# A gated delta net whose four engines issue the same operations in another order

## The reference

```python
def step(S, inp):                       # one token, one head; S is 64 x 128
    qt, kt, vt, bt, gt = inp
    S = S * jnp.exp(gt)[..., None, None]
    kv = jnp.einsum('bhk,bhkv->bhv', kt, S)
    delta = (vt - kv) * bt[..., None]
    S = S + jnp.einsum('bhk,bhv->bhkv', kt, delta)
    ot = jnp.einsum('bhk,bhkv->bhv', qt, S)
    return (S, ot)
```

## Time and profile before

| | us |
|---|---|
| median of three runs | 5250.11 (5246.1 to 5253.67) |
| profiled execution, its own time | 5260.0 |
| its span | 5258.1 |
| PE busy in the span | 4913.4 (93%) |
| POOL, DVE, ACT busy | 3475.1, 3668.1, 3196.8 |
| mean granted TensorE clock | 0.978 of full |

### The profile page before, as it was taken

The page is one execution under the profiler, slowest core; times in us unless marked ns, Lnnn a source line. Parts: engine busy times, 40 slices in busy tenths (PEclk is TensorE's granted clock), DMA queues, the critical chain, the costliest instruction groups (busy, mean ns, idle before and its releaser), DMA issues.

```text
span 5258.1 us, 227335 instructions
## 1 busy us (share of the span) xinstructions
PE 4913.4 (93%) x99564; PEld 3489.0 (66%) x99564; DVE 3668.1 (70%) x5109; ACT 3196.8 (61%) x4833; POOL 3475.1 (66%) x3554
## 2 busy tenths in 40 slices
PE   5999999999999879999999999999999999999998
PEld 3777777777777646666666666666666666665665
DVE  3666666666666567777777777777767776777775
ACT  3666666666666546656655665666655665555554
POOL 2677667676776567666666666776666666766664
PEclk6999999999999989999999999999999999999999
DMA  1000000000000012322222223222222223222222
GB/s 47 3 3 3 8 3 3 7 3 3 3 7 3 31 48 60 81 56 61 63 78 63 65 65 85 64 60 61 59 75 56 65 64 85 64 60 65 60 66 57
DMA packets 154831, 238.86 MB, mean 45 GB/s; under 512 B 42746, under 2 KB 53368, under 8 KB 152952
## 3 DMA queue, kind: packets, MB, share of 16 engines
q1 hardware_dynamic: 153848, 224.32, 16.3%
HBM read 24.96 MB, written 4.19 MB: 6 GB/s over the span
## 4 chain that ended last, share of the span: by engine, by line
PE 77%; ACT 8%; issue 5%; DVE 4%; POOL 4%; POOLq 0%; DVEq 0%; ACTq 0%
PE banks L172 64%; PE banks L176 13%; ACT arena L1997 1%; ACT L2097 1%; POOL arena L2399 1%; ACT arena L2026 1%; DVE arena L1250 1%; DVE arena L2264 1%; DVE arena L2262 1%; DVE arena L2260 1%; DVE arena L2269 1%; ACT arena L2093 1%; ACT arena L2077 1%; ACT arena L2069 1%; ACT arena L2082 1%
## 5 line engine op out<-in xcount | busy, mean ns | idle before, releaser
L172 PE MATMUL banks<-arena 64*32 64x64 f32 (+7 forms) x92652 | 4112.1, 249 | 275.8 <-issue 44.1
L172 PEld LDWEIGHTS banks<-arena 64*64 64x64 f32 (+3 forms) x92652 | 2742.7, 132 | 1414.9 <-issue 914.1
L2369 POOL TENSOR_TENSOR arena<-arena 128x1024 f32<-128x1024 f32 x384 | 903.8, 2363 | 409.9 <-DVE arena L2199 409.9
L176 PE MATMUL banks<-arena 128*128 128x128 f32 x6528 | 911.4, 281 | 62.5 <-POOL arena L2399 22.1
L176 PEld LDWEIGHTS banks<-arena 128*128 128x128 f32 x6528 | 733.1, 143 | 262.3 <-issue 127.4
L2399 POOL TENSOR_TENSOR arena<-arena 128x1024 f32<-128x1024 f32 x384 | 726.3, 1907 | 18.3
L2190 DVE TENSOR_TENSOR arena<-banks,arena 128x1024 f32<-128x1024 f32 x384 | 464.7, 1210 | 248.3 <-ACT arena L1997 230.3
L2406 POOL TENSOR_TENSOR arena<-arena 128x1024 f32<-128x1024 f32 x192 | 369.1, 1922 | 341.4 <-DVE arena L2234 341.3
L2213 DVE TENSOR_REDUCE arena<-banks 128x16 f32<-128x1024 f32 x192 | 235.1, 1224 | 403.5 <-PE banks L172 393.8
L2199 DVE TENSOR_TENSOR arena<-banks,arena 128x512 f32<-128x512 f32 x768 | 491.0, 681 | 0.0
L1199 DVE SCALAR_TENSOR_TENSOR arena<-banks,arena 128x256 f32<-128x256 f32 x768 | 368.5, 480 | 163.6 <-ACT arena L964 134.5
(11 more groups left out here) (136 smaller groups left out, 4546.8 us busy)
## 6 DMA issues: line engine op xcount, KB each, us to landing
arena<-arena SPq DMA_DIRECT2D x1152, 128.0 KB
arena<-arena SPq DMA_DIRECT2D x672, 64.0 KB
arena<-in_Wqkv SPq DMA_DIRECT2D x6, 1536.0 KB, 6.3
arena<-in_Wo SPq DMA_DIRECT2D x6, 512.0 KB
outT<-arena SPq DMA_DIRECT2D x4, 512.0 KB, 2.9
arena<-outT SPq DMA_DIRECT2D x8, 256.0 KB, 4.3
outT<-arena SPq DMA_DIRECT2D x8, 256.0 KB, 2.3
arena<-in_W SPq DMA_DIRECT2D x6, 341.0 KB
```

What stands on the lines that cost most here:

```text
L172: return e.matmul(o, lhsT, rhs, start=start, stop=stop, skip_group_check=True)
L176: return e.transpose(o, i, mat["ident"][0:n, 0:n])
L2369: e.tensor_tensor(T1, T1, T2[i], ALU.add).then_inc(sg(f"g_rope{i}"), 1)
```

## The change

No operation is added, removed or changed, and no buffer either: the lines outside the four lists are identical, and the four bodies keep their counts of calls. The order of the calls in each body is another one, the loop runs one pass more, and where an item of before is named with tiles 2n-3 to 2n+1, it now starts and ends so that up to three tiles are in work at once. The brackets follow the new order.

```diff
-            for n in range(NTILE + 2):
-                tokens_qk(e, 2 * n - 1, 0, [...])
-                level_tr(e, 2 * n - 2, 1, 4, [...])
-                decays_pe(e, 2 * n, [...], [...])
+            for n in range(NTILE + 3):
+                level_y(e, 2 * n - 3, 2, 3, [...])
+                update_state(e, 2 * n - 3, 0, [...])
+                level_tr(e, 2 * n - 3, 2, 3, [...])
```

More of the change, by code:

```diff
@@ L799, in delta_pe @@
[L799 to L802, removed]
@@ new lines, in delta_pe @@
+                project_unit(e, 6 * n, 3)
+                level_y(e, 2 * n - 2, 2, 3, [("v_t1", 2 * n - 1, 0), ("v_h2", 2 * n - 2, 2), ("v_h1", 2 * n - 2, 2), ("v_h5", 2 * n - 2, 1), ("v_h4", 2 * n - 2, 1), ("v_h3", 2 * n - 2, 1)])
+                project_o(e, 2 * n - 3, 2, [("v_np", 2 * n - 1, 1), ("a_kq", 2 * n - 1, 1), ("a_qk", 2 * n - 1, 2), ("a_u", 2 * n - 2, 1), ("x1", 2 * n - 3, 1), ("a_dt", 2 * n, 0)])
+                tokens_v(e, 2 * n - 1, 0, [("v_np", 2 * n - 1, 1), ("a_v0", 2 * n - 2, 2), ("a_u", 2 * n - 2, 1), ("a_kqd", 2 * n - 1, 0), ("a_ot0", 2 * n - 3, 2), ("a_gate", 2 * n - 2, 1), ("a_dt", 2 * n, 0)])
@@ L811, in delta_pe @@
[L811 to L814, removed]
@@ new lines, in delta_pe @@
+                turn_decayed(e, 2 * n - 1, 1, [("a_gate", 2 * n - 2, 2), ("a_v0", 2 * n - 1, 0), ("v_np", 2 * n - 1, 1), ("a_u", 2 * n - 2, 1), ("a_kqd", 2 * n - 1, 0), ("a_ot0", 2 * n - 3, 2), ("a_dt", 2 * n, 0)])
+                project_unit(e, 6 * n + 1, 0)
+                level_y(e, 2 * n - 2, 2, 5, [("v_h1", 2 * n - 1, 0), ("v_h4", 2 * n - 2, 2), ("v_t1", 2 * n - 1, 1), ("v_h3", 2 * n - 2, 2), ("v_h2", 2 * n - 2, 2), ("v_h5", 2 * n - 2, 1)])
+                level_tr(e, 2 * n - 1, 0, 1, [("a_e4", 2 * n - 2, 2), ("a_e3", 2 * n - 2, 2), ("a_e2", 2 * n - 2, 2), ("a_e1", 2 * n - 2, 2), ("a_e5", 2 * n - 2, 1)])
@@ new lines, in delta_pe @@
+                project_o(e, 2 * n - 2, 0, [("a_qk", 2 * n, 0), ("a_u", 2 * n - 2, 2), ("a_kq", 2 * n - 1, 2), ("x1", 2 * n - 3, 2), ("v_np", 2 * n - 1, 1), ("a_dt", 2 * n, 0)])
+                level_y(e, 2 * n - 1, 1, 3, [("v_h3", 2 * n - 1, 0), ("v_h2", 2 * n - 1, 1), ("v_h1", 2 * n - 1, 1), ("v_h5", 2 * n - 2, 2), ("v_h4", 2 * n - 2, 2), ("v_t1", 2 * n - 1, 1)])
+                level_tr(e, 2 * n - 1, 0, 3, [("a_e2", 2 * n - 1, 1), ("a_e1", 2 * n - 1, 1), ("a_e5", 2 * n - 2, 2), ("a_e4", 2 * n - 2, 2), ("a_e3", 2 * n - 2, 2)])
@@ new lines, in delta_pe @@
+                project_g(e, 2 * n - 1, 0, [("v_np", 2 * n - 1, 2), ("a_ot0", 2 * n - 2, 1), ("a_u", 2 * n - 2, 2), ("a_kqd", 2 * n - 1, 1), ("a_gate", 2 * n - 2, 2), ("a_v0", 2 * n - 1, 0), ("a_dt", 2 * n, 0)])
+                level_y(e, 2 * n - 1, 2, 0, [("v_h4", 2 * n - 1, 0), ("v_h3", 2 * n - 1, 1), ("v_h2", 2 * n - 1, 1), ("v_h1", 2 * n - 1, 1), ("v_h5", 2 * n - 2, 2), ("v_t1", 2 * n - 1, 1)])
+                level_tr(e, 2 * n - 1, 0, 4, [("a_e3", 2 * n - 1, 0), ("a_e2", 2 * n - 1, 1), ("a_e1", 2 * n - 1, 1), ("a_e5", 2 * n - 2, 2), ("a_e4", 2 * n - 2, 2)])
@@ L865, in delta_pe @@
[L865 removed]
+                level_tr(e, 2 * n - 1, 1, 4, [("a_e2", 2 * n - 1, 2), ("a_e5", 2 * n - 1, 0), ("a_e1", 2 * n - 1, 2), ("a_e3", 2 * n - 1, 1), ("a_e4", 2 * n - 1, 0)])
                 output_pe(e, 2 * n - 1, 0)
[L867 removed]
@@ L926, in delta_pe @@
-                project_g(e, 2 * n, 0, [("a_ot0", 2 * n - 1, 2), ("a_kqd", 2 * n, 1), ("a_v0", 2 * n, 1), ("a_u", 2 * n - 1, 2), ("v_np", 2 * n, 1), ("a_gate", 2 * n - 1, 2), ("a_dt", 2 * n + 1, 0)])
-                level_tr(e, 2 * n, 1, 2, [("a_e1", 2 * n, 1), ("a_e5", 2 * n, 0), ("a_e4", 2 * n, 0), ("a_e3", 2 * n, 0), ("a_e2", 2 * n, 0)])
-                read_state(e, 2 * n, 0, [("v_state", 2 * n - 1, 2), ("v_og", 2 * n - 1, 2)])
-                project_unit(e, 6 * n + 4, 3)
-                level_y(e, 2 * n, 1, 3, [("v_h2", 2 * n, 1), ("v_h1", 2 * n, 1), ("v_h5", 2 * n, 0), ("v_t1", 2 * n, 1), ("v_h4", 2 * n, 0), ("v_h3", 2 * n, 0)])
@@ L1430, in delta_dve @@
[L1430 to L1441 removed]
+                sum_qk(e, 2 * n - 1, 1)
```

949 lines of the change are left out of this document (473 added, 476 removed).

## The result

| | us |
|---|---|
| before, median of 4 runs | 5251.89 (5246.1 to 5255.58) |
| after, median of 4 runs | 5179.39 (5173.94 to 5184.64) |
| ratio | 0.9863, 95% interval 0.9846 to 0.988 |
| profiled execution after: its time, its span | 5181.43, 5179.6 |

The change takes 72 us off, 1.4%. The page of after, to hold against the earlier trace rows: PE is busy 39 us less, its weight loads 31, ACT 14, POOL 6 us less, and DVE as long as before.

The account below looks back on a forecast made before the run. PE was taken as the bound, waiting at least 7.2 us a period and paying 92 shape changes. Terms summed to -5.3 us a period, 105.8 to 100.5; times 15, -80 us from 5250 gives 5170, range 5132 to 5220.

Parts of the forecast that it names:

- shape changes: Changes of PE tile shape in the body, 92 to 84 at 0.17 us each: -1.3 us a period.
- first place: Behind the first `decays_pe` of a period: waits of 2.4 us fall to 1.0.
- second place: The third group's `level_tr` of levels 1 and 2, straight behind their `level_y`: waits from 1.44 to 0.6 us.
- third place: Behind the second `decays_pe`, where a level's copy now goes ahead of the tables: waits from 2.0 to 0.9 us.
- the rest: Small waits elsewhere, mostly `level_tr` with one operation between it and its `level_y`: 1.4 before, 0.7 us after.
- POOL's `unit_minus` for `level_y(0)` I leave 0.2 late: Behind the first `decays_pe`: a 0.2 us wait on POOL, counted within the 1.0 us remaining there.
- Rival 3: Slower: POOL late for level 0, `unit_minus` behind `scale_kd`, taps and `spread_gate`; 5305 at 1.5 us an item; chance 0.09.
- behind after its table loads: Behind the second `decays_pe`: gaps of 0.53, 0.70 and 1.12 us put to ACT; 2.0 without two weight-shape changes.
- The fill is not longer. I take both as nought.: Ends of the delta net: seven more calls in the drain cost about +1 us; fill and drain counted as nought.
- The weight loads still busy 82: Sign in the profile after: weight loads busy 82 us a period, as before.
- rival 4: The clock: its level in the drain and layers' fill moves the time by 20 us either way; no separate chance.
- Elsewhere 1.00: Mean clock grant outside the drain (0.93) and the 110 us behind the delta net (0.83).

Follow-up runs that it names:

- more_changes: Changed kernel with seven pairs of neighbours exchanged on PE, taking shape changes in the body from 84 to 96; 5221.88 us, ratio 0.9945 to before.
- undo_second: Changed kernel with level_tr(1) and level_tr(2) of the third group's item put straight behind their level_y again; 5210.56 us, ratio 0.9932 to before.
- late_gate: Changed kernel with spread_gate of the odd tiles moved eleven calls later on POOL, behind unit_minus of the second group; 5158.63 us, ratio 0.9821 to before.

## Why the prediction was right, and where it was not

The time, 5179, lies 9 us over the forecast of 5170, and what it names, waits that get cover and fewer shape changes, carried the gain; what it says of the waits' causes holds only in part. By its own terms, in us a period, with the operations' signal times of both kernels for the waits:

| term | forecast | measured |
|---|---|---|
| shape changes, 92 to 84 | -1.3 | -1.4 (8 x 0.17) |
| first place | -1.4 | about -0.4 |
| second place | -0.8 | -1.1 |
| third place | -1.1 | -1.0 |
| the rest | -0.7 | -0.4 |
| sum | -5.3 | -4.8 |

(The measured terms are single operations against the usual time of their kind, by their signals; they add to 4.3, and 0.5 stays unassigned. Runs test the shape changes, the second place and POOL's part of the first; the third place and the rest were undone by no run, and are readings.)

- *Shape changes.* The price and, by more_changes, its place in the sum are right, and so is the count by three shapes.
- *Second place.* Right in kind: 1.65 of waits became 0.57, with the 0.3 on `solve_pe` where it was forecast (0.34). undo_second shows that the order there is worth 2.1 us in the changed kernel.
- *Third place.* 0.40 before `products_pe` on L995 and 0.31 before `update_state`, where they were forecast (as 0.7 and 0.2); a wait of 0.38 before the `level_tr` behind it was not.
- *First place.* This is the step that failed: "POOL's `unit_minus` for `level_y(0)` I leave 0.2 late". It was 1.2 late, and with 0.39 on `silu_gate` (I had 0.7) and 0.34 each on `update_state` and `level_tr`, 2.3 us of waits remain of 2.7. POOL's list gained no time there: late_gate shows what removing it is worth, 1.0 us. Rival 3 named this mechanism with its place, and set against it that "POOL is busy 76 of 105.8 us". That was no argument: in the 30 us that matter POOL is idle for 0.9.
- The cause before was misread as well. The prediction puts 0.86 and 1.18 us of the first place to ACT, and the third place to ACT being "behind after its table loads". The runs without loads show that these cost 0.3 us a period: beside the 0.86 stood DVE's `scale_qk`, and behind the 1.18 POOL.
- *"The fill is not longer. I take both as nought."* The first period has 67 calls on PE where it had 76, and costs 10.1 us less; I counted the calls behind the last unit (7 more) and took them from the periods, when they came out of the fill. From the sixteenth period's start to the end there are 10 calls more, for 1.1 us. This 9 us made good what the periods fell short of (14 x 0.33, and 5 from the first, which I had counted as a full one). That the time came out within 9 us is in part luck, then: an end that I took as nought stood in for a place that gave 1.0 us a period too little.
- "The weight loads still busy 82": they are busy 80.8. 1.6 of the 4.8 us are not in the gaps, from which I had worked out everything. They lie at the breaks in the row of loads, of which there are 20 fewer: about 0.08 us a break that a gap does not show.
- The clock (0.93 in the drain, 0.84 in the layers' start) did not move, and rival 4 gave nothing. "Elsewhere 1.00" was not so: the first period has 0.71 before and 0.72 after.
- By the Trainium skill, "ScalarE: Activation LUTs", What ACT_TABLE_LOAD costs, each load drains ACT for about 1.38 us; the trace does not agree. ACT's timeline at the same first `decays_pe` of the changed kernel, against the earlier trace rows:

```profile
958.14 0.48 ACT L964 ACTIVATE arena<-banks,arena 128x256 f32<-128x256 f32 x1
958.64 1.28 ACT L984 ACT_TABLE_LOAD   x1
959.93 0.81 ACT L987 ACTIVATE arena<-banks 128x768 f32<-128x768 f32 x1
960.76 1.28 ACT L988 ACT_TABLE_LOAD   x1
```

A load follows 0.02 us behind the end of what stands ahead of it and takes 1.28 us, and the next instruction begins 0.01 to 0.02 us behind it: no stretch of 1.38 us stands beside it.

## What to carry to other kernels

An engine's share of a period says nothing on whether it holds the others up: look for the longest stretch in which it has no idle time, and ask who waits for what comes out at its end. Where a wait is named, take the cause away in a run before planning on it, since a second chain may end at the same moment; turning round instructions that are all waited for only moves the wait, while moving one behind them all ends it. And in a hand-written order, an operation pays most where two turn-rounds need it as cover.

## What was not expected of the hardware

- The same `spread_gate` takes 1.49 us or 2.47. In the traces of all fourteen kernels, each of the 59 that took 2.47 ran beside DVE's `scale_qk` (L1215) for 1.1 us, and each of the 389 shorter ones for under 0.8, nearly all for none. In the kernel before these are 15 of 32. In the changed kernel they are three of 32; in eleven other periods the `add_parts` ahead met `scale_qk` instead, and took 1.8 us in place of 0.73. In late_gate it is an `add_parts` in all of these, so that the extra 1 us stayed where it was, and what left the work ahead of `unit_minus` was 1.49 us of `spread_gate` and 0.45 by which `scale_kd` became shorter. No run moved `scale_qk`, so the cause is read from what ran side by side. The place in the changed kernel, then in late_gate:

```profile
964.80 1.70 DVE L1215 TENSOR_TENSOR arena<-arena 128x1024 f32<-128x1024 f32 x1
```

```profile
952.89 2.40 POOL L1450 TENSOR_TENSOR arena<-arena 128x256 f32<-128x256 f32 x2
953.00 1.70 DVE L1215 TENSOR_TENSOR arena<-arena 128x1024 f32<-128x1024 f32 x1
```

- Four table loads of 1.28 us stand in a period of the kernel before. They made the two exponentials signal 1.1 and 0.7 us later, and yet cost 0.3 us of 105.8.
